# One phase of a vision-transformer kernel on one core: when the triangular solves are taken up, where their results are moved, and who adds the read-out

## The reference

```
k    = x / |x|                       # x is the layer-normalised input, per head
v    = (x @ W_write.T) * beta        # beta = sigmoid(x @ W_beta.T)
N    = strictly lower part of -(beta k k^T) * decay
A    = inverse of (I - N)            # a 37 x 37 unit triangular system
o    = lower part of (k k^T * decay) @ (A @ v)
h    = h + x + o @ W_read.T          # W_read joins the two heads
out  = h + router(layernorm(h))      # logits, top expert, expert feed-forward
```

## Time and profile before

| | |
|---|---|
| median of 3 runs | 807.39 us |
| the profiled execution, its own time | 807.8 us |
| its span (first to last instruction) | 806.0 us |
| mean granted TensorE clock | 0.903 |
| PE busy | 677.6 us, 84% |
| DVE busy | 418.5 us, 52% |
| POOL busy | 291.4 us, 36% |
| ACT busy | 247.3 us, 31% |

### The profile page before, as it was taken

The page is one execution under the profiler, slowest core; times in us unless marked ns, Lnnn a source line. Parts: engine busy times, 40 slices in busy tenths (PEclk is TensorE's granted clock), DMA queues, the critical chain, the costliest instruction groups (busy, mean ns, idle before and its releaser), DMA issues. The chain is left out here.

```text
span 806.0 us, 13730 instructions
## 1 busy us (share of the span) xinstructions
PE 677.6 (84%) x4562; PEld 519.1 (64%) x4562; DVE 418.5 (52%) x1120; ACT 247.3 (31%) x679; POOL 291.4 (36%) x483
## 2 busy tenths in 40 slices
PE   5899999999997318999997478793599999999994
PEld 4567776777665217999796367582457676767663
DVE  1567767777775482334697947535333333333331
ACT  0233333333332133444333135452022222223231
POOL 2444444454452000565465736551111212222210
PEclk8899999999997557999899869975589999999998
DMA  8311111011000000000101258296111111111200
GB/s 301 110 36 35 36 36 35 19 35 26 28 1 2 0 0 2 4 8 5 39 7 34 36 113 365 45 366 249 52 44 44 52 47 60 40 59 41 59 26 21
DMA packets 27745, 50.74 MB, mean 63 GB/s; under 512 B 18285, under 2 KB 18415, under 8 KB 27037
## 3 DMA queue, kind: packets, MB, share of 16 engines
q1 hardware_dynamic: 24061, 35.37, 13.9%
q0 software_dynamic: 3328, 10.23, 4.2%
q10 hardware_dynamic: 288, 4.27, 1.3%
HBM read 39.99 MB, written 9.86 MB: 62 GB/s over the span
## 5 line engine op out<-in xcount | busy, mean ns | idle before, releaser
L1890 ACT ACTIVATE work<-psum,cst 128x128 f32<-128x128 f32 x208 | 56.7, 383 | 144.0 <-PE psum L1805 143.9
L1792 PE MATMUL psum<-arena_w,work 128*128 x208 | 95.3, 602 | 1.0 <-DVE work L1844 1.0
L1816 PE MATMUL psum<-arena_w,work 128*128 x416 | 94.2, 379 | 0.4 <-ACT work L1890 0.4
L1816 PEld LDWEIGHTS psum<-arena_w,work 128*128 128x128 f32 x416 | 77.1, 190 | 10.5 <-issue 1.1
L1754 POOL DMA_INDIRECT out<-work,row_i x26 | 25.7, 988 | 159.7 <-DVE work L1866 159.7
L1853 DVE COPY work<-psum 128x512 f32<-128x512 f32 x52 | 36.0, 692 | 69.5 <-PE psum L1792 69.5
L348 PE MATMUL psum<-arena_w 128*111 128x256 f32 x264 | 63.0, 391 | 5.1 <-DMA arena_w<-in_pack 5.1
L713 POOL TENSOR_TENSOR arena_w<-arena_w,work 101x592 f32<-101x592 f32 x33 | 39.5, 1198 | 71.2 <-DVE work L579 71.2
L1792 PEld LDWEIGHTS psum<-arena_w,work 128*128 128x128 f32 x208 | 38.1, 193 | 39.7 <-issue 39.7
L348 PEld LDWEIGHTS psum<-arena_w 128*111 128x111 f32 x264 | 46.0, 180 | 19.2 <-issue 9.8
L704 POOL TENSOR_TENSOR arena_w<-arena_w 128x296 f32<-128x296 f32 x66 | 44.0, 689 | 21.1 <-DVE arena_w L547 21.1
(11 more groups left out here) (218 smaller groups left out, 1335.5 us busy)
## 6 DMA issues: line engine op xcount, KB each, us to landing
arena_w<-in_w SPq DMA_DIRECT2D x2, 4096.0 KB, 13.1
arena_w<-in_x SPq DMA_DIRECT2D x22, 333.0 KB, 2.9
x_rows<-tokens SPq DMA_DIRECT2D x22, 192.0 KB, 4.4
arena_w<-in_pack ACTq DMA_DIRECT2D x1, 2442.0 KB, 10.3
cst<-in_packc ACTq DMA_DIRECT2D x1, 1727.0 KB, 14.4
arena_w<-in_pack SPq DMA_DIRECT2D x1, 818.5 KB, 7.2
arena_w<-in_pack SPq DMA_DIRECT2D x2, 384.0 KB, 4.6
arena_w<-n_rows SPq DMA_DIRECT2D x8, 85.6 KB, 3.0
```

What stands on the lines that cost most here:

```text
L1792: mm = nc.tensor.matmul(bank[2 * j + f][:, :], xgt[j][:, k * 128:(k + 1) * 128], arena_w1[:, bass.ds(expert * (2 * FF) + (k * FF + f * 512 ...
L1816: mm = nc.tensor.matmul(bank[7][:, 0:D], ht[j][:, g * 128:(g + 1) * 128], arena_w2[:, bass.ds(expert * (FC * D) + g * D, D)], start=(g == ...
L1890: nc.scalar.activation(ht[j][:, g * 128:(g + 1) * 128], bank[4 + f][:, k * 128:(k + 1) * 128], ACT.Gelu, bias=cst[:, bass.ds(expert * FC + ...
```

## The change

Seven edits, all in this phase.

1. A group's generator is queued before the third budget of the iteration in which `i - 3` is its last pair, not at the end of the iteration before. The last group's is queued in the second loop at t = 4.
2. `store_inverses(0)` and `load_inverses(0)` come right after the load of group 1, ahead of the stores of tiles 16 to 21.
3. `a_rows` holds both heads of a row side by side (296 B). A group's inverses are loaded in three pieces (first tile, next two, the rest) of two DMAs each: 6 DMAs, where there were 11, 7 and 6.
4. In the last iteration of the first loop PE also solves tiles 0 and 1 and attends tile 0; ACT's copies for them stand there too, ahead of or between the squares and values of the last pair, and POOL spreads their inverses one iteration earlier, ahead of `inverses`. ACT's squares of the last pair move from iteration 11 to iteration 12, behind `copy_solved(0)`.
5. The second loop starts at t = 2 and ends at NT + 4; `turn_outputs`, `router_logits` and their copies follow at a distance of 4 tiles instead of 5, `normalise_outputs` 3 instead of 4, `add_read` 1 instead of 2.
6. `scale_first`, `add_first` and their buffer are gone. DVE adds both halves out of PSUM, one after the other.
7. The second loop's budget is 0.6 instead of 1.1.

```diff
-SLOTS = (0.7, 0.8, 4.2, 1.1)
+SLOTS = (0.7, 0.8, 4.2, 0.6)
...
-    a_rows = nc.dram_tensor("a_rows", (H1, NT * R + RL - R, TOK), F32).ap()
+    a_rows = nc.dram_tensor("a_rows", (NT * R, H1, TOK), F32).ap()
...
+            def loads_of(g):
+                t0, t1 = 2 * GROUPS[g][0], 2 * GROUPS[g][1]
+                return [(t0, t0 + 1), (t0 + 1, t0 + 3), (t0 + 3, t1)]
...
                 def load_inverses(g):
                     sp.wait_ge(a_stored[g], 16 * H1 * group_of(g)[4])
-                    t0, t1 = 2 * GROUPS[g][0], 2 * GROUPS[g][1]
-                    for t in range(t0, t1):
-                        cuts = ROW_CUTS if t == t1 - 1 and g < LAST else ((0, RL),)
-                        for r0, r1 in cuts:
...
+                    for t0, t1 in loads_of(g):
+                        for r0, r1 in ROW_CUTS:
...
+                                         ).then_inc(a_in[t0], 16)
                 for g in range(len(GROUPS)):
                     for t in range(2 * GROUPS[g][0], 2 * GROUPS[g][1]):
                         store_systems(t)
-                        if t == NT - NB and g == LAST > 0:
-                            store_inverses(0)
-                            load_inverses(0)
                     load_systems(g)
+                    if g == LAST - 1:
+                        store_inverses(0)
+                        load_inverses(0)
...
+                    if i == PAIRS + 1:
+                        solve_values(0)
                     row_products(i - 2, 0)
                     outputs(i - 1)
                     hidden(i, range(OC // 2))
+                    if i == PAIRS + 1:
+                        attend(0)
+                        solve_values(1)
                     row_products(i - 2, 1)
...
                 pe.wait_ge(y_added, PAIRS)
-                pe.wait_ge(v_out, NT)
-                pe.wait_ge(n_masked, NT)
-                for t in range(NT + 5):
+                read_out(0)
+                attend(1)
+                for t in range(2, NT + 4):
                     solve_values(t)
                     read_out(t - 1)
-                    turn_outputs(t - 5)
+                    turn_outputs(t - 4)
                     attend(t)
-                    router_logits(t - 5)
+                    router_logits(t - 4)
...
                 for i in range(-1, PAIRS + 2):
                     copy_rows(i - 2)
+                    if i == PAIRS + 1:
+                        copy_solved(0)
+                        squares(i - 2)
                     keep_values(i - 2, 0)
                     activate(i, range(HB // 2))
+                    if i == PAIRS + 1:
+                        copy_attended(0)
+                        copy_solved(1)
                     keep_values(i - 2, 1)
                     copy_gates(i + 1)
                     activate(i, range(HB // 2, HB))
-                    squares(i - 1)
-                for t in range(NT + 5):
-                    normalise_outputs(t - 4)
+                    if i < PAIRS:
+                        squares(i - 1)
+                copy_attended(1)
+                for t in range(2, NT + 4):
+                    normalise_outputs(t - 3)
                     copy_solved(t)
-                    copy_turned(t - 5)
-                    scale_first(t - 1)
+                    copy_turned(t - 4)
                     copy_attended(t)
...
-                    dve.wait_ge(half_added, t + 1)
-                    nc.vector.scalar_tensor_tensor(h, bank[4 + j][0:R, D:2 * D], inv_all[:, t * H1 + 1:t * H1 + 2], h,
-                                                   ALU.mult, ALU.add).then_inc(added, 1)
-                    dve.wait_ge(added, t + 1)
+                    dve.wait_ge(summed, t // 2 + 1)
+                    for k, mark in enumerate((half_added, added)):
+                        nc.vector.scalar_tensor_tensor(h, bank[4 + j][0:R, k * D:(k + 1) * D],
+                                                       inv_all[:, t * H1 + k:t * H1 + k + 1], h,
+                                                       ALU.mult, ALU.add).then_inc(mark, 1)
+                        dve.wait_ge(mark, t + 1)
...
                     decay_products(i - 2, 1)
+                    if i - 3 in ends:
+                        queue.append(substitution(ends[i - 3]))
                     advance(SLOTS[2])
                     if i == PAIRS:
                         identity_columns(LAST)
-                    if i - 2 in ends:
-                        queue.append(substitution(ends[i - 2]))
                 firsts = {2 * p0: g for g, (p0, _) in enumerate(GROUPS)}
-                for t in range(NT + 5):
+                add_read(0)
+                for t in range(2, NT + 4):
+                    if t == 4:
+                        queue.append(substitution(LAST))
                     if t in firsts:
                         advance(math.inf, LAST - firsts[t])
-                    add_read(t - 2)
-                    keep_logits(t - 5)
-                    if t > 0:
-                        advance(SLOTS[3])
+                    add_read(t - 1)
+                    keep_logits(t - 4)
+                    advance(SLOTS[3])
...
                     fold(i - 2, 1)
+                    if i == PAIRS:
+                        spread_inverses(0)
+                        spread_inverses(1)
                     inverses(i - 1)
...
-                for t in range(-2, NT + 2):
-                    power_outputs(t - 2)
-                    add_first(t - 1)
+                for t in range(NT + 2):
                     spread_inverses(t + 2)
+                    power_outputs(t - 1)
```

More of the change, by code:

```diff
@@ L43 @@
 MT = 19
-RL = 112
 GROUPS = ((0, 5), (5, 8), (8, PAIRS))
@@ L887, in build @@
                     "setup"))
[L888 removed]
+            (a_block, vn_done, vn_out, o_done, o_out, r_done, half_added, added, stat2, aggr2, vare2, powered2, normed2,
              turned2, xt_ready, logits, logits_out) = (
                 psem(n) for n in (
[L891 removed]
+                    "a_block", "vn_done", "vn_out", "o_done", "o_out", "r_done", "half_added", "added", "stat2", "aggr2",
                     "vare2", "powered2", "normed2", "turned2", "xt_ready", "logits", "logits_out"))
@@ L926, in build @@
             halves = wc(4, R)
-            first_half = [wc(D, R) for _ in range(2)]
-            ac = arena_w2[0:RL, W2S // 2 + NT * H1 * R:W2S // 2 + NT * H1 * (R + TOK)]
+            ac = arena_w2[0:R, W2S // 2 + NT * H1 * R:W2S // 2 + NT * H1 * (R + TOK)]
             def pair_of(i):
@@ L1170, in turn_outputs @@
                     pe.wait_ge(normed2, t + 1)
+                    if t == 0:
+                        pe.wait_ge(v_out, NT)
+                        pe.wait_ge(n_masked, NT)
                     free(pe, logits_out, t - 1)
@@ L1270, in copy_turned @@
                     nc.scalar.copy(xt[t % 2], bank[6 + t % 2][:, 0:2 * R]).then_inc(xt_ready, 1)
-                def scale_first(t):
-                    if not tile(t):
-                        return
-                    act.wait_ge(r_done, t + 1)
-                    act.wait_ge(inverted, t // 2 + 1)
-                    free(act, half_added, t - 1)
-                    nc.scalar.activation(first_half[t % 2], bank[4 + t % 2][0:R, 0:D], ACT.Copy,
-                                         scale=inv_all[:, t * H1:t * H1 + 1]).then_inc(half_out, 1)
                 def normalise_outputs(t):
@@ L1553, in spread_inverses @@
                         return
-                    pool.wait_ge(a_in[t], 16 * (1 if t not in ends_of_groups else len(ROW_CUTS)))
+                    pool.wait_ge(a_in[load_with[t]], 16 * len(ROW_CUTS))
                     pool.wait_ge(beta_masked, t + 1)
@@ L1569, in power_outputs @@
                     ts(ve2[t % 2][:, 2:3], st2[t % 2][:, 6:7], ve2[t % 2][:, 1:2], -1.0, ALU.mult, ALU.mult).then_inc(powered2, 1)
-                ends_of_groups = [2 * p1_ - 1 for _, p1_ in GROUPS[:LAST]]
+                load_with = {t: t0 for g in range(len(GROUPS)) for t0, t1 in loads_of(g) for t in range(t0, t1)}
                 for i in range(-1, PAIRS + 2):
@@ L1578, in _ @@
                     fold(i - 2, 1)
+                    if i == PAIRS:
+                        spread_inverses(0)
+                        spread_inverses(1)
                     inverses(i - 1)
-                def add_first(t):
-                    if not tile(t):
-                        return
-                    pool.wait_ge(half_out, t + 1)
-                    pool.wait_ge(summed, t // 2 + 1)
-                    tt(h_rows(t), h_rows(t), first_half[t % 2], ALU.add).then_inc(half_added, 1)
-                for t in range(-2, NT + 2):
-                    power_outputs(t - 2)
-                    add_first(t - 1)
+                for t in range(NT + 2):
                     spread_inverses(t + 2)
+                    power_outputs(t - 1)
         with phase():
```

15 lines of the change are left out of this document (6 added, 9 removed).

## The result

The changed kernel takes 795.05 us (median of 4 runs, 793.72 to 795.94) against 807.3 before (805.43 to 808.99): ratio 0.9847, 95% interval 0.9821 to 0.9874. The forecast was 798.7, with 792 to 807 as its range. The profiled execution took 795.94, its span is 794.1, the mean granted clock 0.906.

What follows compares the result with a forecast made beforehand. From iteration 7 on, DVE's order was taken to set the pace. Walking DVE, then PE, put the next phase at 546.1, gain 8.7: span 797.3, plus 1.8 around it, less 0.4 for the median, 798.7 us; range 792 to 807.

Steps and rivals of the forecast that it cites:

- A: First loop, iterations 7 to 10: later preparations lose stalls of 3.33 and 3.96 us; sum 49.1, iteration 11 begins 9.8 earlier.
- B: Iterations 11 and 12: DVE does most steps of group 1, PE begins iteration 12 with tile 0; 20.6 us, to 456.1.
- C: Second loop, tiles 0 to 3: four DVE adds of 1.9 us and three steps of 5.0 in all, ending at 468.7.
- D: Tiles 4 to 14 and group 2: adds, preparation and 18 steps on DVE, 38.7 us; solved at 507.4, against 513.4.
- The rival by which the multiplies wait behind POOL's spreads: Second loop: twelve DVE multiplies wait behind spreads, 6.7 us more, 805.4; one of three equal parts of a 0.18 chance.
- E: Group 2's stores, loads and spread until PE solves tile 16: at 515.3 instead of 521.04, after standing about 12 us.
- F: From PE's solve of tile 16 at 515.3, three tiles at half clock, to the next phase at 546.1; gain 8.7 us.
- the clock: Rival: PE stays at 1.2 GHz from tile 4 to t = 16, 18.6 us more, 817.3; chance 0.11 with other slower courses.
- one of the signs that I had given for being wrong: Second loop: a half-clock stretch of PE between tile 4 and tile 15 would show the forecast wrong.
- The stop did move: No-gain rival: the stop ahead of tile 16 is only moved, 5 to 7 us of gain go, 804 to 806; chance 0.18.
- Faster still: An add's second half costs under 0.52, iteration 10's heavy steps meet less of POOL: 5 to 7 us more, 793; chance 0.11.

Runs made afterwards that it cites:

- the second execution: The changed kernel run once more, with nothing altered, beside other kernels on one chip: 795.13 us.
- budget 2.0: Changed kernel with a budget of 2.0 instead of 0.6 for each tile of the second loop: 786.98 us, ratio to before 0.9768.
- tiles in the drain: Changed kernel with tiles 0 and 1 solved and attended in the second loop, not at the end of the first: 799.05 us, ratio to before 0.9905.
- the 4 MB order: Changed kernel with the 4 MB load of expert weights issued behind the 44 row stores instead of ahead: 793.5 us; with second-loop budget 2.0 as well, 784.22.
- late inverses: Changed kernel with edit 2 undone, group 0's inverses stored and loaded behind the systems of tile 18: 802.31 us beside 795.13 for the change.

## Why the prediction was right, step by step

*A* (49.1): 49.4. The stalls at the preparations went where the rows said. Single iterations were off by up to 0.6 in both directions, so that the sum is better than its parts, and that is luck. Two entries in it I had not counted: the addition at 396.05 took 1.77 instead of 0.83, and the two multiplies of group 0's last step, at 432.40, took 1.97 together where the kernel before has 1.33.

*B* (20.6) and *C* (12.6): 19.5 (437.75 to 457.25) and 11.95. PE came to tile 0 at 58.1 after gate 7 against 58.4 forecast. The loads of the inverses were issued 7.48 us after their stores, not 8.34.

*D* (38.7): 35.8, the term that was mis-sized. I had summed durations. DVE starts an instruction before the one ahead of it has ended (a step's two multiplies at 491.07 last 0.43, and the first reduce starts 0.38 after they began), so from start to start a tile's add, statistics and logits take 1.86, not 1.94 (0.9 over eleven), and the eighteen steps 13.3 instead of 15.5 (2.2). Their durations now sum to 14.7: 0.8 of it is fewer waits, the rest is the overlap. The rival by which the multiplies wait behind POOL's spreads, 6.7 us, did not come: in this stretch POOL's power took 0.80 at 493.74 beside a heavy step, and 0.55 beside the lightest (475.01) and where there was none (512.52), so POOL was the one that waited, as in the earlier trace rows. In the first loop it is once the other way round. This is POOL beside the addition at 396.05:

```profile
396.04 1.09 POOL L1521 TENSOR_TENSOR tokens<-tokens,arena_w 111x512 f32<-111x512 f32 x1
```

DVE's 1.77 is 0.94 more than the 0.83 that the same line took at 471.98, and POOL's add ends 1.08 after DVE's addition began. The Trainium skill, page "SBUF — State Buffer", section "Who interferes with whom", says that whichever starts second waits to the end; by that rule the trace agrees, to 0.14 us. In the pair just ahead it does not: a small POOL operation that took 0.21 at 391.12 began at 395.08, 0.11 before DVE's multiply at 395.19, and it took 1.00 while the multiply took its 0.82. So the starts on record do not settle every pair. The exclusion decided nothing in D: there the spreads of seven tiles (475.88 to 492.25) each began within 0.5 us of the start of an add, which takes its first input from PSUM, and not beside a multiply.

*E* (7.9): 7.6 from the stores to PE (504.99 to 512.62). The stop was 15.55 us, forecast 12.

*F* (30.8): 30.7, by two errors that cancel, which is luck. I had three tiles at half clock, ACT's last normalisation 25.1 after PE's solve of tile 16, and 5.7 from there to the next phase (5.16 and half a microsecond for the rows). In this execution one tile was slow: ACT's last comes after 21.0 (512.62 to 533.65), 4.1 sooner, and the next phase 9.7 after it, 4.0 more than I had. In the second execution both parts came as forecast, 25.1 and 5.7 (511.98, 537.12, 542.81). The end hardly differs, since SP's row stores end at 540.1 and 539.9.

I had worked out this second way to the end and mispriced it. The 545.2 of the prediction is the end of SP's last row issue, 545.6 the issue of the next phase; they are not the same event. In the kernel before the one followed the other by 3.5 (551.26 to 554.80), so the way through the rows gave 548.7, later than the way through ACT by the 3.2 that the prediction states. I counted half a microsecond of it and gave no reason. The rows took 26.96 instead of 29.40, and they set the end; with the 4 MB load behind them they end 1.1 after ACT.

Sum: 0.3 - 1.1 - 0.7 - 2.9 - 0.3 - 0.1 is 4.7 below the forecast, with rounding (159.6 against 154.98 after gate 7), of which 3.65 shows in the medians; 795.05 lies at the lower end of the forecast's own range of 795 to 803. The rivals: the clock did fall twice in the second loop before the stop, for some 3.4 us each, at tiles 2 and 3 (up again by 461.5, before tile 4) and at tile 8 (474.81 to 478.90, 4.09 us). The second is one of the signs that I had given for being wrong, but DVE had no break beside it, and nothing shows that it cost time. The stop did move, from 2.79 to 15.55 us, and the kernel is faster all the same because tile 16 comes earlier (512.62, before 521.04); but the stop was worth 5.9 us after gate 7, 8.2 in the medians, as budget 2.0 shows, and I had costed the burst of the last steps (5.05 us, 499.94 to 504.99) without asking what another budget would give. "Faster still" is what happened, for another reason than the one given.

Not settled: how the 13.4 us split over the edits, beyond what single edits gave (6.5, 4.7, and 3.2 for tiles in the drain, 14.4 together, so they do not simply add). Edit 3 (the layout and the six loads) and edit 7 (budget 0.6 instead of 1.1) had no run of their own; since 2.0 is faster than 0.6, edit 7 may have cost time instead of giving it, which is not shown. Why the 4 MB order gives 4.6 us in the trace and 0 to 2.8 in medians and ratios, and why late inverses cost 7 us in the medians when their trace shows 5.7, is open too; in both cases the profiled execution was the fastest of its kernel.

## What to carry to other kernels

When a wait for a DMA sits in the middle of an in-order engine, ask for its result one iteration later: the stalls of 3.33, 3.96 and 9.85 us went whole, and 6.5 us of it reached the end of the phase. Then read the other end of the same solve: a budget that keeps steps small leaves a lump for the tile that must have them, and a stop of 15 us behind it is only visible as one bracket in PE's timeline. And price a step by the starts of its instructions, not by the sum of their durations, where an engine is busy without a break.

## What was not expected of the hardware

- The granted clock after a stop is not a property of the program: after 15.55 us of idle time the kernel ran one tile in 4.06 us and then 2.57 each, after 15.68 us the same kernel ran three in 4.55, 4.53 and 4.24. From 512.0 to 525.0 of that second execution PE was busy for 13.00 of 13.00 us and its granted clock was 0.50, the lower of the two levels, 1.2 GHz.
- The 44 row stores take 26.5 to 27.7 us behind a 4 MB load (six executions with the DVE add), and 21.1, 22.6 and 24.8 ahead of it. Waits for ACT are part of both, but with ACT done at 524.1 they still ran until 531.5 (budget 2.0). The larger stores (192 KB) landed after a median of 2.8 us in the change, 3.5 in its second execution and 3.7 with budget 2.0, and after 2.1 in all three with the load behind them.
